# Attention and gated feed-forward block on one core: more probability buffers in the first tile, and moved steps in the loop

## The reference

```
qkv = x @ w_qkv.T;  q, k rotated by RoPE tables
attn = softmax(mask(q k^T * scale));  o = attn @ v;  a = o @ w_out.T
x1 = layernorm(x + a)
gate = silu((x1 @ w_gate) * s_gate);  up = (x1 @ w_up) * s_up
out = layernorm(x1 + ((gate * up) @ w_down) * s_down)
```

## Time and profile before

| | before |
|---|---|
| median of 3 runs | 1297.01 us (1289.78 to 1300.4) |
| profiled execution, device time | 1294.35 us |
| its span, first to last instruction | 1292.5 us |
| mean granted clock of PE | 0.970 |
| PE busy | 1212.9 us (94%) |
| DVE busy | 970.7 us (75%) |
| ACT busy | 571.3 us (44%) |
| POOL busy | 377.1 us (29%) |

### The profile page before, as it was taken

One profiled execution on the slowest core, in us unless ns is written; L12 is line 12 of the kernel. 1 busy time (PEld: TensorE's weight loads), 2 busy tenths in 40 slices (PEclk: granted clock), 3 DMA queues, 4 the chain that ended last, 5 costly groups with the idle time before them and its releaser, 6 DMA issues.

```text
span 1292.5 us, 24588 instructions
## 1 busy us (share of the span) xinstructions
PE 1212.9 (94%) x8200; PEld 548.4 (42%) x8200; DVE 970.7 (75%) x2797; ACT 571.3 (44%) x1608; POOL 377.1 (29%) x370
## 2 busy tenths in 40 slices
PE   8624999999999999999999999999999999999997
PEld 3212444444444444444444444444444444444443
DVE  6855799757997489965897669975799658996543
ACT  1464168502774038810586017840388205870230
POOL 1032115410353104521055102441045210551331
PEclk9855999999999999999999999999999999999999
DMA  9953484334654265441943337542655508443000
GB/s 328 231 109 68 98 151 95 78 64 91 123 95 90 51 114 99 99 86 41 160 101 60 78 80 134 98 87 42 117 107 96 95 34 158 100 65 71 33 1 33
DMA packets 345912, 124.74 MB, mean 97 GB/s; under 512 B 309056, under 2 KB 329792, under 8 KB 345792
## 3 DMA queue, kind: packets, MB, share of 16 engines
q1 hardware_dynamic: 337776, 108.32, 43.9%
q10 hardware_dynamic: 4896, 8.52, 1.8%
q0 software_dynamic: 3120, 6.29, 1.6%
HBM read 27.67 MB, written 8.39 MB: 28 GB/s over the span
## 4 chain that ended last, share of the span: by engine, by line
PE 40%; issue 28%; POOL 11%; DVE 9%; DMA 4%; ACT 4%; SPq 3%; POOLq 0%; DVEq 0%; ACTq 0%
PE bank L420 31%; PE bank L523 6%; POOL xT_sb L363 5%; POOL fuse L368 4%; DMA xT_sb<-xT_sb 2%; DVE fuse L705 2%; PE bank L491 2%; ACT probs L630 2%; DVE fuse L721 1%; SPq L282 1%; DMA qkT<-fuse 1%; DVE largest L833 1%; SPq L288 1%; PE bank L471 1%; POOL x L380 1%
## 5 line engine op out<-in xcount | busy, mean ns | idle before, releaser
L420 PE MATMUL bank<-wqkv,xT_sb 128*128 128x512 f32 x760 | 332.8, 598 | 1.1 <-DMA wqkv<-w_qkvT 0.8
L363 POOL TENSOR_TENSOR xT_sb<-probs,xT_sb 128x512 f16<-128x512 f32 x120 | 142.5, 1187 | 487.1 <-ACT xT_sb L588 487.1
L630 ACT ACTIVATE probs<-bank,neg_max,qk_scale 128x128 f32<-128x128 f32 x512 | 227.2, 455 | 71.1 <-DVE neg_max L761 51.1
L420 PE MATMUL bank<-x1T,wg 128*128 128x512 f16 (+1 forms) x1032 | 243.0, 378 | 0.9 <-DVE ffn_tmp L768 0.9
L420 PE MATMUL bank<-x1T,wu 128*128 128x512 f16 x1024 | 241.9, 379 | 0.0
L588 ACT ACTIVATE fuse<-fuse 128x512 f16<-128x512 f32 x128 | 70.0, 617 | 360.0 <-DVE fuse L711 351.9
L523 PE MATMUL bank<-wd,fuse 128*128 128x512 f16 x1024 | 222.3, 379 | 0.0
L420 PEld LDWEIGHTS bank<-wqkv,xT_sb 128*128 128x128 f32 x760 | 144.0, 191 | 181.4 <-issue 179.1
L368 POOL TENSOR_TENSOR fuse<-ffn_tmp,fuse 128x512 f16<-128x512 f32 x128 | 152.9, 1194 | 71.0 <-ACT fuse L588 69.2
L523 PEld LDWEIGHTS bank<-wd,fuse 128*128 128x128 f16 x1024 | 100.2, 98 | 123.1 <-issue 4.0
L420 PEld LDWEIGHTS bank<-x1T,wu 128*128 128x128 f16 x1024 | 100.2, 98 | 120.6
(11 more groups left out here) (95 smaller groups left out, 1018.8 us busy)
## 6 DMA issues: line engine op xcount, KB each, us to landing
xT_sb<-xT SPq DMA_DIRECT2D x36, 256.0 KB, 4.1
v_cross<-v_own SPq DMA_DIRECT2D x64, 128.0 KB, 2.6
qkT<-x SPq DMA_DIRECT2D x8, 1024.0 KB, 5.8
out<-y ACTq DMA_DIRECT2D x32, 256.0 KB, 2.3
wqkv<-w_qkvT SPq DMA_DIRECT2D x2, 1024.0 KB, 7.2
wd<-w_down POOLq DMA_DIRECT2D x1, 2048.0 KB, 10.7
wg<-w_gate POOLq DMA_DIRECT2D x1, 2048.0 KB, 14.3
wu<-w_up POOLq DMA_DIRECT2D x1, 2048.0 KB, 18.8
```

Source lines behind the costliest of these rows:

```text
L363: done(probs_low, pool.tensor_tensor(place[:, 1, :, :], probs[:, s % 2, :, :], place[:, 0, :, :], ALU.subtract))
L420: last = pe.matmul(dst, lhsT, rhs, start=(i == 0), stop=(i == len(pairs) - 1))
L630: last = act.activation(probs[:, s % 2, h, :], src, ACT.Exp, bias=neg_max[:, s % 2, h:h + 1], scale=qk_scale[:, 2:3], accum_out=row_sum[:, ...
```

## The change

- Probability buffers: `probs_place` gives in the first tile four fp32 places (two in `probs`, two in `ffn_tmp`, free there), in the loop two as before. The split halves have two places in every tile (before: four in the first tile). `exponentials(s)` in the first tile waits for `probs_low(s - 4)`; in every tile it waits for `sum_inverted(s - 2)` too.
- Step 0 in the loop: DVE does `weights(0)` before `split_v(3)`; ACT does `keep_probs_high(0)` right after `gate_tanh(0)` instead of behind `exponentials(1)`; SP issues `turn_probs(0)` and `turn_probs(1)` ahead of `cross_v(2)` and `cross_v(3)`.
- The rows of x come in four DMAs of 256 KB, after steps 6, 7, 8 and 9.
- Tile end: `weigh_v(14)` and `weigh_v(15)` come one projection later; `down(0)` comes before `project_o(3)`; DVE does `keep_o(7)` after `split_x1(0)`, and in the loop `tile_maximum` and `start_y(0)` before the steps of block 3; POOL spreads the maximum before the last `rstd1`.

```diff
-        more_places = [halves(ffn_tmp[:, i, :]) for i in range(2)]
+        def probs_place(s, ffn):
+            if ffn or s % 4 < 2:
+                return probs[:, s % 2, :, :]
+            return ffn_tmp[:, s % 2, :].rearrange("p (h c) -> p h c", h=HG)
...
 SP
+            def load_rows(a, j):
+                if j == 0:
+                    wait(scores_done, sp, a, 2 * NG - 1)
+                sp.dma_start(x_rows[:, j, :], x[bass.ds(a * TILE + j * P, P), :]).then_inc(rows_in, 16)
...
                         turn_qk(a, j)
-                        if j:
+                        if 1 <= j < NB - 1:
                             cross_v(a, j - 1)
-                    cross_v(a, NB - 1)
                     for s in range(STEPS):
                         turn_probs(a, s, ffn)
-                        if s == 2 * NG - 2:
-                            wait(scores_done, sp, a, 2 * NG - 1)
-                            sp.dma_start(x_rows, tile_rows(a)).then_inc(rows_in, 16)
+                        if s < 2:
+                            cross_v(a, NB - 2 + s)
+                        if 0 <= s - (2 * NG - 2) < NB:
+                            load_rows(a, s - (2 * NG - 2))
...
 POOL
                         done(rstd1, pool.tensor_tensor(rstd[:, i:i + 1], ...))
-                    if ffn:
-                        spread_maximum(a)
+                        if ffn and j == NB - 2:
+                            spread_maximum(a)
...
 PE
-                    for j in range(NB):
-                        project_o(a, j, ffn)
-                        if j < 2:
-                            weigh_v(a, STEPS - 2 + j)
-                if ffn:
-                    for j in range(NB):
+                    project_o(a, 0, ffn)
+                    project_o(a, 1, ffn)
+                    weigh_v(a, STEPS - 2)
+                    project_o(a, 2, ffn)
+                    weigh_v(a, STEPS - 1)
+                if ffn:
+                    down(f, 0, attn)
+                if attn:
+                    project_o(a, NB - 1, ffn)
+                if ffn:
+                    for j in range(1, NB):
                         down(f, j, attn)
...
 ACT
-            def exponentials(a, s):
+            def exponentials(a, s, ffn):
                 wait(bias_done, act, a, s)
-                wait(probs_low, act, a, s - 2)
+                wait(probs_low, act, a, s - 2 if ffn else s - 4)
+                wait(sum_inverted, act, a, s - 2)
...
-                if ffn and s >= 2:
+                if s >= 2:
                     wait_probsT(act, a, s - 2)
-                elif s >= 4:
-                    wait_probsT(act, a, s - 4)
...
-                        keep_probs_high(a, s - 1, ffn)
+                        if s >= 2 or not ffn:
+                            keep_probs_high(a, s - 1, ffn)
                     if ffn:
                         gate_tanh(f, s)
...
+                        if attn and s == 0:
+                            keep_probs_high(a, s, ffn)
...
 DVE
+                    if ffn:
+                        weights(a, 0, ffn)
                     split_v(a, NB - 1)
...
-                        weights(a, s)
+                        if s or not ffn:
+                            weights(a, s, ffn)
...
-                    for j in range(NB + 2):
-                        if j < NB:
-                            start_x1(a, j)
-                        if j == 0:
-                            keep_o(a, STEPS // 2 - 1)
-                        if 1 <= j <= NB:
-                            finish_x1(a, j - 1)
-                        if j >= 2:
-                            split_x1(a, j - 2)
+                    start_x1(a, 0)
+                    start_x1(a, 1)
+                    finish_x1(a, 0)
+                    start_x1(a, 2)
+                    split_x1(a, 0)
+                    keep_o(a, STEPS // 2 - 1)
+                    finish_x1(a, 1)
+                    split_x1(a, 1)
+                    finish_x1(a, 2)
+                    split_x1(a, 2)
                     if ffn:
                         tile_maximum(a, ffn)
+                        start_y(f, 0)
+                    start_x1(a, NB - 1)
+                    finish_x1(a, NB - 1)
+                    split_x1(a, NB - 1)
+                    next_scales(a)
+                elif ffn:
                     start_y(f, 0)
-                if attn:
-                    next_scales(a)
                 if ffn:
                     for j in range(1, NB):
                         start_y(f, j)
                         finish_y(f, j - 1)
```

More of the change, by code:

```diff
@@ L221, in build @@
         s_raw = ffn_tmp[:, 0, 0:2 * STEPS]
-        def tile_rows(a):
-            return x[bass.ds(a * TILE, TILE), :].rearrange("(b p) n -> p b n", p=P)
         def wait_qkT(eng, a, j):
@@ L244, in wait_v_cross @@
             wait(v_cross_in[j], eng, a, 31)
-        def split_place(s, ffn):
-            return split_places[s % 2] if ffn else (split_places + more_places)[s % 4]
+        def probs_place(s, ffn):
+            if ffn or s % 4 < 2:
+                return probs[:, s % 2, :, :]
+            return ffn_tmp[:, s % 2, :].rearrange("p (h c) -> p h c", h=HG)
         def bodies(eng, body):
@@ L296, in turn_probs @@
                 sp.dma_start_transpose(probsT[s % 2].rearrange("p z h c -> p (z h) c"),
-                                       split_place(s, ffn).rearrange("p z h c -> p (z h c)"))\
+                                       split_places[s % 2].rearrange("p z h c -> p (z h c)"))\
                     .then_inc(probsT_in[s % 2][0], 16)
@@ L361, in split_probs @@
                 wait(probs_high, pool, a, s)
-                place = split_place(s, ffn)
-                done(probs_low, pool.tensor_tensor(place[:, 1, :, :], probs[:, s % 2, :, :], place[:, 0, :, :],
+                place = split_places[s % 2]
+                done(probs_low, pool.tensor_tensor(place[:, 1, :, :], probs_place(s, ffn), place[:, 0, :, :],
                                                    ALU.subtract))
@@ L623, in keep_v @@
                                   v_scale[:, 1:2]))
-            def exponentials(a, s):
+            def exponentials(a, s, ffn):
                 wait(bias_done, act, a, s)
-                wait(probs_low, act, a, s - 2)
+                wait(probs_low, act, a, s - 2 if ffn else s - 4)
+                wait(sum_inverted, act, a, s - 2)
                 for h in range(HG):
                     src = bank32[S_BANKS[s % 2]][:, h * P:(h + 1) * P]
-                    last = act.activation(probs[:, s % 2, h, :], src, ACT.Exp,
+                    last = act.activation(probs_place(s, ffn)[:, h, :], src, ACT.Exp,
                                           bias=neg_max[:, s % 2, h:h + 1], scale=qk_scale[:, 2:3],
@@ L637, in keep_probs_high @@
                     wait(v_done, act, a, NB - 1)
-                if ffn and s >= 2:
+                if s >= 2:
                     wait_probsT(act, a, s - 2)
-                elif s >= 4:
-                    wait_probsT(act, a, s - 4)
                 wait(probs_ready, act, a, s)
-                done(probs_high, copy(split_place(s, ffn)[:, 0, :, :], probs[:, s % 2, :, :]))
+                done(probs_high, copy(split_places[s % 2][:, 0, :, :], probs_place(s, ffn)))
             def body(t, attn, ffn):
@@ L655, in body @@
                     keep_v(a, 2, ffn)
-                    exponentials(a, 0)
+                    exponentials(a, 0, ffn)
                     keep_v(a, 3, ffn)
@@ L660, in body @@
                     if attn and s:
-                        exponentials(a, s)
-                        keep_probs_high(a, s - 1, ffn)
+                        exponentials(a, s, ffn)
+                        if s >= 2 or not ffn:
+                            keep_probs_high(a, s - 1, ffn)
                     if ffn:
@@ L729, in split_v, with weights @@
                                                       op0=ALU.mult, op1=ALU.subtract))
-            def weights(a, s):
+            def weights(a, s, ffn):
                 wait(exp_done, dve, a, s)
@@ L735, in weights @@
                 inverse = free_view(inv_sum[:, s % 2, :], [[1, HG], [0, P]])
-                rows = probs[:, s % 2, :, :]
+                rows = probs_place(s, ffn)
                 done(probs_ready, dve.scalar_tensor_tensor(out=rows, in0=rows, scalar=2.0 ** PROB_BITS, in1=inverse,
@@ L791, in start_x1 @@
                 if j == 0:
-                    dve.wait_ge(rows_in, (a + 1) * 16)
+                    dve.wait_ge(rows_in, (a + 1) * 16 * NB)
                 add_x(a, j)
```

## The result

The changed kernel takes 1321.53 us (median of four runs, 1320.93 to 1322.26), the kernel before in the same runs 1297.86 us: ratio 1.0193, 95% interval 1.0148 to 1.0239 (the two medians alone give 1.018). The prediction was 1313 us, range 1301 to 1330. The profiled execution took 1321.23 us against 1294.35, a difference of 26.9 us, which the traces divide as follows.

What follows compares the result with a forecast made beforehand. PE was taken as the bound wherever it does not wait (busy 1212.9 of 1292.5 us). The terms sum to +16.1 us on the profiled 1294.35, 1310.5 us; that execution lying 2.7 us below the median, 1313 us was predicted, range 1301 to 1330.

Steps and rivals of the forecast that it cites:

- the forecast as summed: Whole kernel: all terms added, +16.1 us on the profiled execution; given a chance of 0.55.
- the first rival: Before `down(3)`: PE falls to 1.2 GHz in every body, 17 us more, 1330 us; chance 0.13.
- Tile 0, the steps: First tile's exponentials: four buffers end ACT's wait behind POOL, 2.98 us a step instead of 3.91, -12 us.
- Tile 0, the end: `project_o(3)` of tile 0 waits for the later `keep_o(7)`, +7.3 us, then runs at a slow clock, +2.4 us.
- The end of a loop body: `down(3)` starts 2.8 to 3.5 us late, POOL's spread delaying the last root: 3.2 us in seven bodies, +22.4 us.
- The second rival: Loop body's end: POOL isn't held behind the spread, `down(3)` never waits, 1286 us; chance 0.12.
- No loss of clock at `down(3)`: PE's idle of some 3 us before `down(3)` leaves matmuls at full speed, no loss.
- Step 0: Loop, `weigh_v` of step 0: an earlier transpose removes the stall in all seven bodies, -8.4 us.
- The late tail: DVE's later tail delays scores in six bodies, +3 us, and gate(2) in the last body, +1.4 us.

Runs made afterwards that it cites:

- the two kernels shown under the clock: The new tile end alone on the kernel before, 1331.64 us; and the changed kernel with `keep_o(7)` ahead of `finish_x1(0)` in tile 0, 1314.82 us.
- the filling: The changed kernel with 12 extra matmuls, their result unused, in PE's idle before `down(3)`: 1314.72 us, ratio 1.0122 to the kernel before.

## Why the prediction was right, and where it was off

The direction and its main cause, the wait of `down(3)` behind POOL's spread, came out. The size lies in the range, 8.5 us above the point that was forecast, and in part by luck: two terms were 18.0 us too low, and the others together 7.2 us too high. The case that came about is not the forecast as summed, but for most of it the first rival, the fall of the clock, which had a chance of 0.13. Step by step:

- **Tile 0, the steps (-12 us): right.** The last `weigh_v` of step 13 starts at 107.28 instead of 119.40 us, 12.1 earlier. Two steps take 5.96 us (2.27 or 2.28, then 3.68), so 2.98 each, as forecast. The four loads of x have a share that the prediction gave them only inside its bounds: with the four buffers alone it was 10.5 us. ACT's Exp now waits for DVE's bias, no longer for POOL:

```profile
85.20 0.46 ACT L639 ACTIVATE probs<-bank,neg_max,qk_scale 128x128 f32<-128x128 f32 x1 [1.29 <-DVE neg_max L771]
```

- **Tile 0, the end (+7.3 and +2.4): right in place and cause.** The wait is 7.87 us, and the slow clock cost 1.57 us instead of 2.4; undoing it let tile 1 start 9.1 us earlier.
- **The end of a loop body (+22.4): right in place and cause, 20.9 us measured.** The forecast had `down(3)` start 38.5 to 39.2 us behind `project_o(0)`; in tile 1 it started 38.5 us behind, in all seven 38.2 to 39.5. The root after the spread ended at 34.3 us (34.2 to 34.9 forecast). The second rival, in which POOL isn't held behind the spread, is out.
- **No loss of clock at `down(3)`: the step that failed.** I took the nearer row, the idle of 2.37 us at the start of a tile, and gave the loss 0.13. It occurred in six bodies of seven, 10.0 us of busy time. The first rival's price of 17 us was too high for this kernel, since `down(3)` lost 1.69 us at most and not 2.4; with the new tile end alone it lost 2.83 and 2.93 us in two bodies. The idles of the six were 2.78 to 3.84 us, that of the seventh 2.50 us, but no length parts the two cases: in the two kernels shown under the clock an idle of 3.43 us cost nothing. Taking the nearer row by its length was the mistake. Where two rows lie at 2.37 and 5 us and the forecast is 3.2, neither settles it, and the answer "none" was a choice that the rows didn't support.
- **Step 0 (-8.4): mis-sized, -2.8 net.** The waits at step 0 went, as forecast. The prediction took each stall as PE time that comes back, and had nothing on what the loop does with it: new stalls of `weigh_v` came in later steps, in bodies with 6 stretched `weights` each, 42 in all instead of 25. By itself, on the kernel before, the part brought nothing (ratio 1.0016).
- **The late tail (+3 and +1.4): the second right and covered, the first not seen.** In the last body gate(2) waited less than before, 0.51 us:

```profile
1236.46 1.90 PE L423 MATMUL bank<-x1T,wg 128*128 128x512 f16 x8 [0.51 <-DVE ffn_tmp L778]
```

  The forecast was 0.94 + 1.3. With the clock kept by the filling it is 2.2 us, as forecast, and 2.2 us too with `keep_o(7)` early, where the last `down(3)` of the loop happens to keep the clock; in the changed kernel that `down(3)` takes 1.7 us longer, and DVE's tail is hidden behind that. For the same reason the clock's loss cost less than its busy time in that one body. The 3 us at `scores` did not come, with the filling neither. The kernel with the spread last has 3.6 us of them in its loop.

The forecast's sum was +16.1 us, the execution's +26.9. The down products add 12.4 us and step 0 adds 5.6; `scores` with the rest takes 3.5 off, the last body 1.9, the wait at `down(3)` 1.5 and tile 0 0.3: 10.8 us.

## What to carry to other kernels

Ask of every operation of an engine not only when its input is ready, but what the instruction ahead of it keeps the engine for: the record of POOL's spread is 0.41 us, and the next instruction comes 7 us later. A wait that is put before a burst of matmuls costs its own length, and it can cost the clock too, in some bodies and not in others; price both, and don't read the second from the length of the idle alone. And when stalls of a loop disappear while its time doesn't, compare the mean duration of the same instruction between bodies: here DVE, held up beside POOL, showed it as a longer instruction (1.52 us instead of 0.69), in no list of waits.

## What the runs showed of the hardware

- A DVE instruction with two inputs in SBUF (128x512, fp32) takes 0.69 us, and 1.52, in a few cases up to 1.67, when POOL's subtraction runs (1.15 us). Splitting that subtraction in two brought 1.0% on the kernel before.
- After idles of PE of 2.78 to 3.84 us in the loop `down(3)` took 8.59 or 8.77 us, in tile 1 at a granted clock of 0.81; after the one of 2.50 us it took 7.08. The length of the idle does not tell the loss: the longest one, 3.84 us, cost the least of the six, and in two other kernels one of 3.43 us cost nothing and one of 3.39 us 2.93 us. 12 matmuls in the idle kept `down(3)` at 7.08 us in all seven bodies, and the granted clock at 1.00 in tile 1.
- POOL's spread over partitions holds it for some 13 us at the end of a body: in tile 1 of the changed kernel 6.17 from its input to its record, and 7.07 from there to the next instruction's start, although that one's input was ready. In the seven bodies of the kernels before and after these are 6.0 to 6.6 and 7.1 to 7.6 us.
